# TensorE's order in a unit of two attentions: the side piece ahead of the second part of the odd step's product

## The reference

```
x = L0_attn_x
xn = _layernorm(x, axis=-1)
s = _L0_attn_ref(xn, ...)          # LayerNorm, qkv, softmax(q k / sqrt(8)) v, out projection, + residual
g = _silu(_L0_ffn_ref(xn, ...))    # square(relu(xn W_fc)) W_proj, then 5 spiking steps
x = x + s * g
xn = _layernorm(x, axis=-1)
s = _L1_attn_ref(xn, ...)          # causal attention with ALiBi slopes
g = _silu(_L1_ffn_ref(xn, ...))    # 3 rounds of a small coupling network
x = x + s * g
```

## Time and profile before

| | us |
|---|---|
| median of 3 runs | 959.24 |
| profiled execution, time | 960.38 |
| profiled execution, span | 958.6 |
| TensorE matmuls busy | 811.0 (85%) |
| ScalarE busy | 836.5 (87%) |
| VectorE busy | 412.2 (43%) |
| POOL busy | 178.3 (19%) |
| TensorE clock granted, mean | 0.963 |

### The profile page before, as it was taken

How to read it: one execution, slowest core, us unless ns; L and a number is a source line. 1 busy time by engine, 2 the same in 40 slices (tenths; PEclk the granted TensorE clock), 3 DMA queues, 4 the chain that set the end, 5 groups by cost and what they waited for, 6 DMA issues and landing times. The chain is left out here.

```text
span 958.6 us, 23599 instructions
## 1 busy us (share of the span) xinstructions
PE 811.0 (85%) x10046; PEld 329.2 (34%) x10046; DVE 412.2 (43%) x874; ACT 836.5 (87%) x951; POOL 178.3 (19%) x218
## 2 busy tenths in 40 slices
PE   2847999899999999999999988837778788888876
PEld 1412333333343433433334342213233333333332
DVE  7632244635457554574455776771112111121222
ACT  5736999999999999999999955638999999999995
POOL 1101110103112031111311111001223232233132
PEclk9777999999999999999999999978999999999998
DMA  6773020020200302003001042010202102012000
GB/s 173 242 242 86 2 69 5 1 72 2 71 25 23 116 1 72 29 19 116 2 1 40 30 139 84 0 45 1 71 1 83 57 27 82 27 57 83 13 1 23
DMA packets 32050, 53.55 MB, mean 56 GB/s; under 512 B 5576, under 2 KB 16456, under 8 KB 31944
## 3 DMA queue, kind: packets, MB, share of 16 engines
q1 hardware_dynamic: 31944, 52.02, 17.2%
HBM read 31.29 MB, written 20.71 MB: 54 GB/s over the span
## 5 line engine op out<-in xcount | busy, mean ns | idle before, releaser
L938 ACT ACTIVATE a_probs<-a_sc 128x1024 f32<-128x1024 f32 x512 | 474.5, 1032 | 19.1 <-PE a_sc L1129 18.6
L1805 ACT ACTIVATE a_probs<-a_sc 128x1024 f32<-128x1024 f32 (+1 forms) x320 | 274.7, 958 | 35.0 <-PE a_sc L1932 20.3
L1144 PE MATMUL a_o<-a_probs,vt 128*18 128x256 f32 (+1 forms) x3072 | 271.4, 456 | 0.0
L1129 PE MATMUL a_sc<-q_st,k_st 32*128 32x512 f32 x1024 | 131.4, 501 | 26.2 <-ACT a_probs L938 17.6
L1967 PE MATMUL a_o<-a_probs,vt 128*18 128x256 f32 (+3 forms) x1920 | 153.3, 429 | 0.0
L1926 PE MATMUL a_sc<-q_st,k_st 32*128 32x512 f32 (+3 forms) x768 | 80.7, 427 | 66.6 <-ACT a_probs L1805 54.6
L1144 PEld LDWEIGHTS a_o<-a_probs,vt 128*18 128x18 f32 x3072 | 65.3, 97 | 143.4 <-issue 103.5
L1129 PEld LDWEIGHTS a_sc<-q_st,k_st 32*128 32x128 f32 x1024 | 50.6, 183 | 140.6 <-ACT a_probs L938 127.9
L1831 POOL TENSOR_SCALAR_AFFINE_SELECT a_probs<-a_probs 128x512 f32<-128x512 f32 x96 | 59.7, 643 | 208.4 <-ACT a_probs L1805 208.4
L1926 PEld LDWEIGHTS a_sc<-q_st,k_st 32*128 32x128 f32 x768 | 38.0, 184 | 131.4 <-ACT a_probs L1805 115.6
L1853 DVE STREAM_TRANSPOSE a_turn<-a_o 128x512 f32<-128x512 f32 x16 | 11.5, 717 | 151.2 <-PE a_o L1967 151.2
(11 more groups left out here) (231 smaller groups left out, 754.7 us busy)
## 6 DMA issues: line engine op xcount, KB each, us to landing
q_st<-q_hl SPq DMA_DIRECT2D x48, 256.0 KB
k_st<-k_hl SPq DMA_DIRECT2D x48, 256.0 KB
q_hl<-parts SPq DMA_DIRECT2D x12, 512.0 KB, 4.4
k_hl<-parts SPq DMA_DIRECT2D x12, 512.0 KB, 4.8
q_hl<-p_parts SPq DMA_DIRECT2D x4, 512.0 KB, 4.1
k_hl<-p_parts SPq DMA_DIRECT2D x4, 512.0 KB, 5.1
out_dram<-x SPq DMA_DIRECT2D x7, 256.0 KB, 4.5
x<-in_L_attn_x_dram SPq DMA_DIRECT2D x3, 512.0 KB, 6.0
```

The source lines that it names most:

```text
L938: nc.scalar.activation(probs[t % RING][:, 2 * pair:2 * pair + 2, :], scores[unit % SLOTS][:, :, :], ACT.Exp).then_inc(expd, 1)
L1129: ins = nc.tensor.matmul(scores[(2 * t + i // 2) % SLOTS][:, i % 2, :], k_st[part, g, kt * P:(kt + 1) * P], q_st[part, g, qh * HALF:(qh + ...
L1144: ins = nc.tensor.matmul(o_ps[32 * h:32 * h + 2 * W9, c0:c1], vt[b % 2][:, kt, gp, h, W9 * gs:W9 * gs + 2 * W9], probs[t % RING][:, h, c0: ...
L1805: nc.scalar.activation(probs[t % RING][:, 2 * pair:2 * pair + 2, 0:width(t)], scores[unit % SLOTS][:, :, 0:width(t)], ACT.Exp).then_inc(ex ...
```

## The change

In both attentions the loop that writes TensorE's list issues the unit's side piece before the second part of the odd step's product, where it issued it after that. All else stays: the instructions, their waits, and the lists of the other engines.

```diff
@@ first_attention
                 for pair in range(LAST):
                     if 2 * pair < S:
                         score(2 * pair)
+                    for one in pieces_at(pair):
+                        piece_of(*one)
                     if 0 <= 2 * pair - 1 - LAG < S:
                         product(2 * pair - 1 - LAG, CUT, HALF)
-                    for one in pieces_at(pair):
-                        piece_of(*one)
                     if 2 * pair < S:
                         score(2 * pair + 1)
                     if 0 <= 2 * pair - LAG < S:
```

## The result

| | us |
|---|---|
| before, median of 4 runs | 959.36 (958.57 to 960.07) |
| after, median of 4 runs | 967.62 (966.71 to 970.66) |
| ratio, 95% interval | 1.0092 (1.0068 to 1.0116) |
| forecast, range | 969.3, 964.5 to 971.8 |

What follows compares the result with a forecast made beforehand. ScalarE's exponentials looked like the bound, but in units with a side piece TensorE's chain was slightly longer (3.72 against 3.67 us). Terms 8.9 + 0.6 + 0.8 - 0.2 = 10.1 on 959.24 gave 969.3 us, range 964.5 to 971.8.

Steps and rivals of the forecast that it cites:

- rival A: At the 12 ends only the product waits, the side bank's copy being through in time: 965.8 us; chance 0.10.
- the start: Third unit of the first attention: the second part comes behind a side piece that waits for VectorE; 0.6 us lost.
- the ends: 12 first-attention units with a side piece where VectorE transposes the output bank after 16 steps: 8.9 us lost.
- the second attention: Gain of at most 0.11 us in 4 units with the second `z`, less 7 slower `mix` pieces: -0.2 us.
- product waits for the transpose: At the 12 ends the next product starts late: 0.55 us for `fc` and `v0`, 0.35 for `xt`.
- late weight loads: Short matmuls of `y`, `mix`, `v0`, `v1` lose their loads' 0.21 us head start: 58 pieces x 0.014, 0.8 us.
- Nothing in TensorE's chain to give: First-attention units with a side piece: TensorE's chain is slightly longer than ScalarE's, so delays above some 0.05 us are lost.
- rival B: First attention: ScalarE has work in hand, so late products at the 12 ends cost nothing: 959.2 to 960 us; chance 0.07.
- rival C: First attention: change of tile hidden, ends absorbed, side units fall to ScalarE's 3.67 us: 955 us; chance 0.04.
- The hand-over from VectorE to TensorE: At the ends, the delay from VectorE's transpose to TensorE's product: taken as 0.1 us, between 0.05 and 0.15.
- The second wait: Behind an end, the next unit's side piece waits for VectorE's late copy of the side bank: 0.28 us for `fc`.
- What would show it: Trace signs: end transposes start at 2.0 or 1.7 us, new waits for VectorE, L938's idle time 19 to some 28 us.

Runs made afterwards that it cites:

- e_ends: before with the new order only in the first attention's units in which an end is due; 964.78 against 960.04 us, ratio 1.0057.
- e_next: after with the old order in each first-attention unit that follows an end unit; 965.61 against 960.26 us, ratio 1.0048.
- e_zmove: before with the second z piece of each batch in unit 8 instead of 6, order unchanged; 960.20 against 960.26 us, ratio 0.9997.

## Why the prediction was right, point by point

The direction, the place and the mechanism were right, and the sum, 10.1, lies inside the measured interval (6.5 to 11.1 us). The times alone would not have shown that: the median, 967.6, lies midway between the forecast (969.3) and rival A (965.8), and A's 6.6 is inside the interval too. The trace tells them apart. There B and E together are 8.9 longer; of the 1.2 that the sum has more, 0.6 is the start, 0.3 the ends (8.6 instead of 8.9) and some 0.2 the second attention. By its terms, measured from the starts of scores in the trace after against before:

| term | predicted | measured |
|---|---|---|
| product waits for the transpose, 4 `fc` | 4 x 0.55 | 4 x 0.57 |
| the same, 6 `xt` | 6 x 0.35 | 5 x 0.37 and once 0.18 |
| the same, 2 `v0` | 2 x 0.55 | 2 x 0.53 |
| side piece behind waits for the copy | 3 x 0.28, 6 x 0.32, 2 x 0.38 | 3 x 0.27, 6 x 0.28, 2 x 0.38 |
| late weight loads | 0.8 | 0.8 |
| the start | 0.6 | -0.2 (A) |
| second attention | -0.2 | -0.45 (E) |

- *The one `xt` end with 0.18*: the next unit starts 3.99 behind, as in the others, but before it already started at 3.81 there instead of 3.63, in both traces of before. The prediction took all six alike.
- *Nothing in TensorE's chain to give*: right, by the starts of units. The 0.20 of idle time that it also named as a shrunken wait for an exponential is no such wait, as the 0.42 in the same place of after shows. A lateness of 0.57 is a lateness of 0.57 at the last step; B grows by the plain sum of the waits, 5.4 + 3.2 + 0.8 = 9.4. ScalarE has no work in hand (rival B), and of rival C nothing is seen: units with `y` became 0.01 longer, not shorter.
- *The hand-over from VectorE to TensorE*, taken as 0.1 for the product: 0.12 to the loads and 0.15 to the matmuls (265.19 to 265.31 and 265.34). For the side piece 0.06 (266.74 + 0.65 = 267.39 to 267.45) against 0.05.
- *The second wait*: the size was right, its ownership was not stated. The prediction priced "an end unit", and named the earlier claim on the bank (4.13 against 4.04) without saying in which unit it arises. e_ends and e_next show that the unit behind it must have the new order as well. Rival A (only the product waits) describes not after, but e_ends.
- *Late weight loads*: the sum is right and the account is half right. I had 58 pieces of short matmuls at 0.014 and none for the 44 with 512 columns. Measured are 0.01 for each unit, `fc` and `k` included (28 `fc` units: 0.33 in all, 28 `y` units: 0.26). The weight loads of `fc` start with their matmuls too now (262.91 both), where before they started 0.22 ahead (260.96 against 261.18). That this late start is what costs the 0.01 is read from the rows; no experiment changes it alone.
- *The start*: the second part does come behind the waiting side piece now, and takes 1.01 us at half clock (timeline of after, against the earlier trace rows):

```profile
83.46 0.75 DVE L1077 TENSOR_TENSOR vt<-a_side,bv 128x256 f32<-128x256 f32 x2
...
84.27 1.94 PE L123 MATMUL a_side<-w,y 128*32 128x128 f32 x32 [5.64 <-DVE vt L1077]
85.97 1.08 PE L1144 MATMUL a_o<-a_probs,vt 128*18 128x256 f32 x8
...
86.98 0.68 PE L1129 MATMUL a_sc<-q_st,k_st 32*128 32x512 f32 x4
87.59 1.49 PE L1144 MATMUL a_o<-a_probs,vt 128*18 128x512 f32 x16
```

  But the clock is back at the full level by the next product (1.49 long, where the trace before has 2.77 at half clock), and A is no longer than before. Over the ten traces, A has a mean of 23.3 in the five with the old order in the third unit and 23.9 in the five with the new one. The 0.6 may be real, but single values of both kinds lie between 22.4 and 24.4, so it isn't shown.
- *Second attention*: one gain was missing. A change of tile gone was put at 0.11 at most, and it gave 0.09, but the second `z` won 0.14: the earlier loads of its transposes, 0.05, were not in the sum. The `mix` pieces lost too little to be seen.
- *The range*: its upper bound lies 2.5 above the forecast, where the bounds named for it (1.2, 0.3, 0.8) make 2.3, and its lower bound rests on holding rival A as well.
- *What would show it*: all rows came as named (transpose at 2.0 and 1.7, PE a_o <- DVE a_turn, PE a_side <- VectorE's copies), except that the releaser of the product behind `xt` is given as ScalarE. The idle time of L938 grew to 26.6, not 28.

## What to carry to other kernels

When a piece of work is moved behind another on one engine, ask what the moved piece is the last input of, and who waits for that: here 0.44 us of matmuls were the last input of a 0.72 us transpose, which lay beside the side piece for nothing and now lies on the path, twelve times. A late result costs twice when its consumer works in order: once for what waits for it directly, and once for what waits behind it on the consumer's queue, but the second cost is paid only if the next user wants its buffer early, so a reordering that is made in all units can cost more than the sum of its parts. And where a chain has no slack, count it from start to start in a few units before trusting an idle-time total: 19 us of idle time over some 490 us hid units that were already 0.05 us on the wrong side.

## What the runs showed of the hardware

The end of the kernel runs at either level of TensorE's clock, in one and the same program. Windows of the last `tail` pieces (the row gives the stretch, busy us of each engine, and behind POOL the granted clock), after and after once more:

```profile
955.50:960.50 5.00, 1.90 (x56) 1.17 (x48) 2.81 (x6) 0.00 (x0) 0.00 (x0) 1.00 0.01 3
```

```profile
959.10:964.10 5.00, 2.52 (x44) 2.07 (x48) 2.69 (x7) 0.00 (x0) 0.00 (x0) 0.70 0.01 3
```

The first `tail` piece takes 1.08 us in the one and 1.93 in the other. In both it follows 2.6 us in which TensorE waited for VectorE. Stretches with such waits (A, C, D, F) hold nearly all of what differs between two traces of one kernel, up to 1.6 us each, while 460 us of dense work repeat within 0.1 us. That they hold the spread of the timed runs too is likely, but those have no traces. For a change worth under 0.2% the starts of one instruction group, compared between two traces over the dense stretch, say more than a dozen timed runs did here (e_zmove).
